# Edge counts of a graph layer in ten blocks of 125x125 a tile, three chunks a visit

## The reference

```
h = (x @ W.T).reshape(n, heads, out_ch)
e = leaky_relu(a_src[src] + a_dst[dst], 0.2)
m = segment_max(e, dst);  ex = exp(e - m[dst]);  denom = segment_sum(ex, dst)
out = segment_sum(ex / (denom[dst] + EPS) * h[src], dst)
x = x + gat2(relu(gat1(layernorm(x))));  x = x + ffn(layernorm(x))
```

## Time and profile before

| | us |
|---|---|
| median of 3 runs | 711.22 (710.97 to 712.07) |
| the profiled execution | 711.5 |
| its span | 709.7 |
| PE busy | 698.6 (98%) |
| DVE busy | 528.8 (75%) |
| ACT busy | 439.1 (62%) |
| POOL busy | 146.9 (21%) |

### The profile page before, as it was taken

The page is one execution under the profiler, slowest core; times in us unless marked ns, Lnnn a source line. Parts: engine busy times, 40 slices in busy tenths (PEclk is TensorE's granted clock), DMA queues, the critical chain, the costliest instruction groups (busy, mean ns, idle before and its releaser), DMA issues.

```text
span 709.7 us, 13757 instructions
## 1 busy us (share of the span) xinstructions
PE 698.6 (98%) x4705; PEld 655.6 (92%) x4705; DVE 528.8 (75%) x864; ACT 439.1 (62%) x898; POOL 146.9 (21%) x136
## 2 busy tenths in 40 slices
PE   8899999999999999999999999999999999999997
PEld 6699999888999999999999999999999899999997
DVE  5999888698999999999999664445568752737232
ACT  4665584387999999999999754553453333522202
POOL 2558121000112112121221000000223331323202
PEclk9999999999999999999999999999999999999999
DMA  8627887658633433443411431101882634315102
GB/s 285 215 69 199 255 249 218 183 148 247 199 71 76 94 69 84 81 99 59 92 21 21 123 116 59 59 0 37 253 276 64 207 92 189 102 57 178 44 23 66
DMA packets 48178, 88.35 MB, mean 124 GB/s; under 512 B 5263, under 2 KB 30831, under 8 KB 48128
## 3 DMA queue, kind: packets, MB, share of 16 engines
q1 hardware_dynamic: 37548, 65.69, 31.3%
q0 software_dynamic: 6080, 8.17, 7.4%
q10 hardware_dynamic: 4500, 13.82, 5.9%
HBM read 68.09 MB, written 15.33 MB: 118 GB/s over the span
## 4 chain that ended last, share of the span: by engine, by line
PE 90%; DVE 4%; DMA 4%; ACT 1%; issue 1%; POOL 0%; ACTq 0%; SPq 0%; DVEq 0%
PE bank L1479 19%; PE bank L1619 13%; PE bank L1440 12%; PE bank L1543 12%; PE bank L1336 11%; PE bank L1723 4%; DMA w1n_sb<-in_W 3%; PE bank L1695 3%; PE bank L1251 3%; PE bank L1597 2%; PE bank L1749 1%; DVE x2f L2359 1%; PE bank L1486 1%; PE bank L1485 1%; ACT w_hi L1035 1%; PE bank L1253 1%
## 5 line engine op out<-in xcount | busy, mean ns | idle before, releaser
L1479 PE MATMUL bank<-PT,h1s 125*128 125x250 f32 x660 | 147.5, 374 | 0.0
L1479 PEld LDWEIGHTS bank<-PT,h1s 125*128 125x128 f32 x660 | 121.2, 190 | 13.6
L2124 DVE SCALAR_TENSOR_TENSOR L<-asb,nad 125x1250 f32<-125x1250 f32 x80 | 121.3, 1551 | 2.5 <-DMA asb<-src_logit_rows 1.7
L2135 DVE CUSTOM_DVE_ANT_0 L<-L,LC 125x1250 f32<-125x1250 f32 x80 | 113.7, 1452 | 1.3
L950 ACT ACTIVATE L<-L,nm 125x1250 f32<-125x1250 f32 x80 | 109.7, 1373 | 7.1 <-DVE nm L2135 5.8
L1440 PE MATMUL bank<-ident,L 125*125 125x125 f32 x800 | 94.0, 273 | 0.0
L1440 PEld LDWEIGHTS bank<-ident,L 125*125 125x125 f32 x800 | 91.1, 189 | 0.8 <-issue 0.4
L971 ACT COPY PT<-bank 125x500 f32<-125x500 f32 x165 | 83.8, 616 | 1.9 <-PE bank L1440 1.9
L767 POOL DMA_DIRECT2D PT_diff<-PT x34 | 28.4, 836 | 157.9 <-ACT PT L971 157.9
L1932 DVE TENSOR_TENSOR hotr<-iota,r 125x1500 f16<-125x1500 f16 x50 | 46.6, 932 | 8.1 <-PE bank L1253 4.5
L1619 PE MATMUL bank<-h_hi,PT_hi 125*125 125x384 f32 x200 | 41.5, 350 | 0.0
(11 more groups left out here) (288 smaller groups left out, 1419.9 us busy)
## 6 DMA issues: line engine op xcount, KB each, us to landing
asb<-src_logit_rows SPq DMA_DIRECT2D x14, 416.5 KB, 3.5
atom_w<-in_atom_inT SPq DMA_DIRECT2D x5, 1152.0 KB, 12.6
atom_w<-in_atom_outT SPq DMA_DIRECT2D x5, 1152.0 KB, 9.7
log_count_scratch<-LCw SPq DMA_DIRECT2D x10, 546.9 KB
LC<-log_count_scratch SPq DMA_DIRECT2D x10, 546.9 KB
LCt<-log_count_scratch SPq DMA_DIRECT2D x10, 546.9 KB
h_scratch<-h1st ACTq DMA_DIRECT2D x10, 448.0 KB
PT_diff<-PT POOLq DMA_DIRECT2D x34, 122.1 KB, 3.0
```

The lines of the kernel that those rows point to most:

```text
L1479: mm = pe.matmul(sums, h1s[q][:, s, :], PT[p][:, s, :], start=(s == (0 if plain else PART + 2)), stop=(plain and s == NT - 1))
L2124: dve.scalar_tensor_tensor(L[s % RING][:, :], asb[q][0:NP, 1, :], nad1[:, ds(h, 1), t:t + 1].rearrange("p h t -> p (h t)"), asb[q][0:NP, 0 ...
L2135: dve.tensor_tensor_reduce(out=L[s % RING][:, :], in0=L[s % RING][:, :], in1=LC[:, t, :], scale=-1.0, scalar=-FLOOR, op0=ALU.add, op1=ALU.min,
```

## The change

A tile now has 10 blocks of 12 or 13 targets (`SUB` = 10; neighbours share the target at an odd edge), with row number target in block times 10 plus source divided by 125, and column number source modulo 125. Each block's counts are 125x125, a quarter of a bank. A visit makes two pairs of chunks and uses three of the four (`TRIP` = 2, `VISIT` = 3). The two tables become one, `edges`, one copy per tile parity, with four fp16 per chunk: row and column number, each of the chunk and of the chunk behind it. So a read may begin at any chunk, and the odd case on TensorE is gone. A block's first chunk is written as its place at even spread (`PLACE`) plus an offset of 0 to 3 chunks, two bits a block in the plan instead of four. The semaphores of the one-hots go by pairs of blocks (`HW` = 5). The count store writes 10 pieces of 125 numbers a partition. GpSimd fills both tables with -1 at the start; VectorE fills the row numbers twice per tile (`rows_of_edges`), and behind the one-hots of tile 0 also the column numbers of the second table.

```diff
-SUB = 5
+SUB = 10
+HW = SUB // 2
-WD = N // NW
-TRIP = 3
+WD = 13
+TRIP = 2
 VISIT = 2 * TRIP - 1
+PLACE = [w * NE // (CE * NW) for w in range(SUB)]
+LEAD = 16
-COLS = 2 * NCH + 4
+COLS = 2 * NCH + LEAD + 2
...
-        r16 = sb("r16", [CE, COLS], F16, p1)
-        g16 = [sb(f"g16_{p}", [CE, COLS], F16, p1) for p in range(2)]
-        hotk = [sb(f"hotk{w}", [CE, TRIP, NP, 2], F16, p1) for w in range(SUB)]
-        hotr = [sb(f"hotr{w}", [CE, TRIP, GW, 2], F16, p1) for w in range(SUB)]
+        edges = [None, sb("edges1", [CE, COLS, 2, 2], F16, p1)]
+        hot = [sb(f"hot{w}", [CE, 2, TRIP, NP, 2], F16, p1) for w in range(SUB)]
...
             for w in range(SUB):
-                pool.memset(sixteens[:, w:w + 1], float(16 ** w)).then_inc(consts_made, 1)
+                pool.memset(place[:, w:w + 1], float(PLACE[w])).then_inc(consts_made, 1)
+            for w in range(SUB):
+                pool.memset(fours[:, w:w + 1], float(4 ** w)).then_inc(consts_made, 1)
             for j in range(2):
                 pool.iota(iota2[:, :, j], pattern=[[1, SUB * NP]], ...)
...
+            for t in range(2):
+                pool.memset(edges[t][:, :, :, :], -1.0).then_inc(blank_set, 1)
...
                 with pe.Fori(0, count) as c:
-                    for w in range(SUB):
-                        out = bank[w // 2][0:NP, (w % 2) * GW:(w % 2 + 1) * GW]
-                        odd = ((start + (aways >> (4 * w)) + c) & 1).with_bounds(min_val=0, max_val=1)
-                        pe.wait_ge(hot_ready[w], before + c + 1)
-                        for q, j in ((0, 1), (1, 0), (1, 1), (2, 0)):
-                            pe.matmul(out, hotk[w][:, q, :, j], hotr[w][:, q, :, j], start=False, stop=True,
-                                      skip_group_check=True)
-                        mm = pe.matmul(out, end_of(hotk[w], odd), end_of(hotr[w], odd), start=False, stop=True,
-                                       skip_group_check=True)
-                        mm.then_inc(hot_used[w], 1)
+                    for v in range(HW):
+                        pe.wait_ge(hot_ready[v], before + c + 1)
+                        for w in (2 * v, 2 * v + 1):
+                            out = bank[w // 4][0:NP, (w % 4) * NP:(w % 4 + 1) * NP]
+                            for q, j in ((0, 0), (0, 1), (1, 0)):
+                                mm = pe.matmul(out, hot[w][:, 1, q, :, j], hot[w][:, 0, q, :, j], start=False, stop=True,
+                                               skip_group_check=True)
+                        mm.then_inc(hot_used[v], 1)
...
+            def place_of(t, kind, j):
+                return edges[t % 2][:, LEAD - j:LEAD - j + NCH, kind, j]
+
+            def rows_of_edges(t):
+                for j in range(2):
+                    s = dve.tensor_scalar(place_of(t, 1, j), gcol[:, :], -float(t * N), None, ALU.add)
+                s.then_inc(rows_set, 1)
...
                 with dve.Fori(0, count) as c:
-                    for w in range(SUB):
-                        away = ((aways >> (4 * w)) & 15).with_bounds(min_val=0, max_val=15)
-                        pair = ((start + away + VISIT * c) >> 1).with_bounds(min_val=0, max_val=COLS // 2 - TRIP)
-                        dve.wait_ge(hot_used[w], before + c + 1)
-                        dve.tensor_tensor(hotr[w][:, :, :, :],
-                                          iota2[:, 0:GW, :].unsqueeze(1).to_broadcast([CE, TRIP, GW, 2]),
-                                          r16[:, ds(2 * pair, 2 * TRIP)].rearrange("p (q j) -> p q j", j=2)
-                                          .unsqueeze(2).to_broadcast([CE, TRIP, GW, 2]), ALU.is_equal)
-                        dve.tensor_tensor(hotk[w][:, :, :, :],
-                                          iota2[:, w * NP:(w + 1) * NP, :].unsqueeze(1).to_broadcast([CE, TRIP, NP, 2]),
-                                          g16[t % 2][:, ds(2 * pair, 2 * TRIP)].rearrange("p (q j) -> p q j", j=2)
-                                          .unsqueeze(2).to_broadcast([CE, TRIP, NP, 2]), ALU.is_equal
-                                          ).then_inc(hot_ready[w], 1)
+                    for v in range(HW):
+                        dve.wait_ge(hot_used[v], before + c + 1)
+                        for w in (2 * v, 2 * v + 1):
+                            at = start + ((aways >> (2 * w)) & 3) + VISIT * c + PLACE[w]
+                            chunks = ds(at.with_bounds(min_val=0, max_val=COLS - 2 * TRIP), 2 * TRIP)
+                            for kind in range(2):
+                                made = dve.tensor_tensor(
+                                    hot[w][:, kind, :, :, :],
+                                    iota2[:, kind * w * NP:(kind * w + 1) * NP, :].unsqueeze(1).to_broadcast([CE, TRIP, NP, 2]),
+                                    edges[t % 2][:, chunks, kind, :].rearrange("p (q e) j -> p q e j", e=2)[:, :, 0, :]
+                                    .unsqueeze(2).to_broadcast([CE, TRIP, NP, 2]), ALU.is_equal)
+                        made.then_inc(hot_ready[v], 1)
+                if t == 0:
+                    dve.scalar_tensor_tensor(gcol[:, :], dstf[:, :], float(SUB), qc[:, :], ALU.mult, ALU.add
+                                             ).then_inc(edge_step, 1)
+                    for j in range(2):
+                        dve.scalar_tensor_tensor(place_of(1, 0, j), qc[:, :], -float(NP), srcf[:, :], ALU.mult, ALU.add)
+                    dve.wait_ge(edge_step, 5)
                 if t + 1 < NT:
-                    local_rows(t + 1)
+                    rows_of_edges(t + 1)
                     return plan_of(t + 1)
```

More of the change, by code:

```diff
@@ L252, in gnn_ffn_kernel @@
         vv = sb("vv", [NS, 2 * NW], F32, early)
-        vm = sb("vm", [2 * NW, 1], F32, early)
-        sixteens = sb("sixteens", [1, SUB], F32, early)
+        vm = sb("vm", [NW, 2], F32, early)
+        fours = sb("fours", [1, SUB], F32, early)
+        place = sb("place", [1, SUB], F32, early)
         nf = sb("nf", [1, NT, SUB], F32, early)
+        ends = sb("ends", [1, NT, SUB], F32, early)
         st = sb("st", [1, NT], F32, early)
@@ L297, in gnn_ffn_kernel @@
         xT_lo = [sb(f"xT_lo{p}", [128, KD, NP], F32R, p1) for p in range(2)]
-        xT_first = sb("xT_first", [128, KD, NP], F32, p1)
-        h1st = [sb(f"h1st{p}", [NP, HC], F32, p1) for p in range(2)]
+        edges[0] = sb("edges0", [CE, COLS, 2, 2], F16, p1)
+        pad_edges = sb("pad_edges", [CE, 32], F32, p1)
+        h1st = [sb("h1st0", [NP, HC], F32, p1)]
+        whole = ExitStack()
+        xT_first = sb("xT_first", [128, KD, NP], F32, whole)
+        whole.close()
+        h1st.append(sb("h1st1", [NP, HC], F32, p1))
         rows1 = sb("rows1", [H, 2, N], F32, p1)
@@ L411, in gnn_ffn_kernel @@
             sem(n) for n in ("span_step", "span_turned", "edge_step", "plan_ready"))
-        plan_step, g16_set = sem("plan_step"), sem("g16_set")
-        hot_ready = [sem(f"hot_ready{w}") for w in range(SUB)]
-        hot_used = [sem(f"hot_used{w}") for w in range(SUB)]
+        plan_step, rows_set, blank_set = sem("plan_step"), sem("rows_set"), sem("blank_set")
+        hot_ready = [sem(f"hot_ready{v}") for v in range(HW)]
+        hot_used = [sem(f"hot_used{v}") for v in range(HW)]
         cnt_full, ln_done, lc_done = (sem(n) for n in ("cnt_full", "ln_done", "lc_done"))
@@ L1902, in _ @@
             then(dve.scalar_tensor_tensor(trip[:, :], run[4][:, 8:18], 64.0, run[0][:, 9:19], ALU.mult, ALU.add))
[L1903 to L1904 removed]
+            then(dve.scalar_tensor_tensor(trip2[:, :], st[:, :], -2.0 ** 16, trip[:, :], ALU.mult, ALU.add))
             then(dve.tensor_tensor(offw[:, :, :], off[1][:, :, :],
[L1906 removed]
```

93 lines of the change are left out of this document (46 added, 47 removed).

## The result

The changed kernel takes 728.22 us (728.05 to 728.56, 4 runs) against 711.64 us (710.97 to 712.44, 4 runs): ratio 1.0233, 95% interval 1.0215 to 1.0251. It is slower by 16.6 us, where 8 us less had been forecast. The profiled execution has a span of 726.2 us.

A forecast was written before the change was run, and what follows sets the result against it. TensorE was taken to bound the kernel, VectorE close behind. 711.5 us less 9.6 for rounds and count 9, plus 1.5 for the later start, gave 703.4, or 703.1 against the median; range 699.8 to 710.3.

The forecast's parts named there:

- Counts: TensorE's count of a tile: 30 matmuls of 125 columns at 0.060 us, 2.0 us in all, 1.2 less than the mean.
- the rival with 0.081: TensorE's count matmuls run at the skill's distance of 0.081 us, rounds of 9.98, total 707.6 us; chance 0.12.
- One-hots: VectorE's one-hot loop: twenty instructions at 0.33 us, 6.55 a tile, nothing gained or lost; register work hides by 0.04 a block.
- Rounds: Eight rounds from count 1 to count 9: 9.40 us each instead of 10.56, a gain of 9.3 us.
- Start: VectorE's path to `wrow1` 2.6 us later, making TensorE's L1393 begin 1.5 later; bounds 0.5 and 3 us.
- GpSimd late with its two fills: At the start, doubled `iota2` and two memsets stand before `blank_set`, for which VectorE waits; a case for the 3 us bound.
- The upper bound of 3 us: Most that the later start was to cost TensorE, where 1.5 us was taken.
- GpSimd is starved: Rival: VectorE's gaps shrink, GpSimd's root for tile 8 holds up a turn once, up to 9 us; chance 0.06.
- the new row instructions may leave the access open: Reason against starved GpSimd: VectorE's new row-number instructions might let GpSimd into SBUF; no size given.
- Stores: Count stores in 1250 pieces of 500 bytes instead of 625 of 1000: DMA share 0.9 instead of 0.70, still hidden.
- the bound of 0.053: Count stores: a packet of 500 bytes was taken to last as long as one of 1000, 0.053 us.
- No second visit: One-hot blocks: each needs one visit as before; a second would cost its tile another 6.5 us of VectorE.

The follow-up runs named there:

- h_var: The changed kernel with each tile's variance and the scaled mean of tiles 8 and 9 computed by ScalarE instead of GpSimd: 713.48 us.
- o_added: `i_fast` with one tiny VectorE instruction, result unused, added behind `rows_of` of tiles 0 and 1: 704.84 us, ratio 0.9912.
- i_fast: `h_var` and `a_fill` together, with the second copy of `iota2` made by ScalarE and VectorE's work for tile 1 moved behind `watt1`: 715.74 us.
- a_fill: The changed kernel with GpSimd's two fills of the edge tables given to VectorE: 724.27 us.
- d_held_before: The kernel before, with four fills of 1250 numbers a partition added behind GpSimd's start-up work: 715.01 us, ratio 1.0039.
- n_gate_nmr: The changed kernel with eight VectorE waits for GpSimd's roots and one more for tile 8's scaled mean: 721.24 us.
- p_apart: `i_fast` with `rows_of` and `column_scaled` set apart on VectorE in the rounds of tiles 3 and 5 to 7: 720.45 us, ratio 1.0109.

## Why the prediction was wrong, point by point

- *Counts.* Forecast 0.060 us a pair and 2.0 a count. Measured 1.82 us for 30 pairs (53.10 to 54.92), 0.061, and 2.00 from 52.95 to 54.95. Right; the rival with 0.081 is out.
- *One-hots.* 0.33 apart and 6.55 a tile; measured 6.58 (54.77 to 61.35). No time to "issue" within the loop, so the register work hides. Right. (The elements per block fell to 1000 from 2250, four ninths and not the two fifths said under the change.)
- *Rounds.* 9.40, 75 to 76 us for eight. Measured 9.34 in the undisturbed ones, 75.8 in `h_var`, 75.94 in `o_added`. Right.
- *Start.* The path to `wrow1` was to be 2.6 later. It ends at 39.08 instead of 32.96, 6.1 later. The hold of L1857 is 3.5 of it (its successor begins at 8.80, in `i_fast` at 5.29), and 2.6 remain. That this equals the forecast is in part luck: VectorE begins L2059, the former L2038, 6.75 later, so the items took 3.2 (1.7 instead of 0.9 up to the one-hots of tile 0, 1.5 instead of 1.7 behind them), and 0.6 of it filled a wait that VectorE had for TensorE before L2042. The item that was missing is larger: "GpSimd late with its two fills" was thought of as VectorE waiting for `blank_set`, which was set in time. The fills did not have to be late to cost something: they kept GpSimd's queue unbroken while VectorE wanted in. That made 3.5 us on the path, and the lower clock behind TensorE's longer wait 4.5 more. Measured: 10.15 later at count 1, where 1.5 was taken. The upper bound of 3 us had no clock in it, though an idle TensorE was part of it.
- *GpSimd is starved.* This was the mechanism, and it had a chance of 0.06 and the price of one stall of 5 us. It was two stalls and 16.6 us. The step that failed is the reason against it, that "the same root under an idle moment took 0.55": the question was how many idle moments would be left. Before, VectorE waited for TensorE 0.76 to 1.77 us in each round from 75.73 on, and the one long root (44.37) falls into the stretch without such a wait. The forecast itself closed these waits, with both engines at 9.4, and still took the gain in full. The hope that "the new row instructions may leave the access open" was wrong as well: L720 waited from 52.27 past those at 61.35. The price counted one instruction late once; a tile needs two or three, and three in a row lost a round each (9.75, 9.44 and 9.77 us from 95.44 on).
- *Stores.* A store of 1237 packets took 49.9% of the 16 engines over 5 us (55 to 60), 0.032 us a packet of 500 bytes, less than the 0.053 of one of 1000, but a fifth more for the same bytes (66.5 us of engine time a MB instead of 55.6). The stage's DMA share is 0.80 and no engine waits for a store. Right that they hide; the bound of 0.053 was above the truth.
- *No second visit*: x30 in each of the counts. Right.

So 9.7 us of rounds were gained as forecast and 26.8 lost, 10.2 at the start and 16.6 in the rounds. The 16.6 are GpSimd's. Of the 10.2, 1.5 had been forecast from VectorE's own new work; 5.3 went in `a_fill` with 2.5 of the 3.5 us of hold. That VectorE and GpSimd shut each other out, and that this costs the time, is shown by `a_fill` and `d_held_before` for the start and by `h_var`, `n_gate_nmr`, `p_apart` and `o_added` for the rounds.

The Trainium skill (SBUF — State Buffer, Who interferes with whom) says that VectorE and GpSimd share a pair of ports, that an instruction of VectorE with two inputs from SBUF contends with a GpSimd instruction that reads there, and that the second to come is blocked until the first has finished. The trace agrees for the roots, which wait under one-hots with two inputs, that one is blocked, but not for how long: 19.25 and 39.6 us are dozens of VectorE's instructions of 0.4 us. These sentences do not cover the start: L1857 has one tensor as input and the fills have none, and yet it was held for 3.9 us, over five of GpSimd's instructions. So a queue without a break is often not entered between two of its instructions.

Often, not always. GpSimd in the kernel before, and VectorE beside it:

```profile
65.86 1.13 POOL L708 TENSOR_TENSOR rstd<-var,powers 125x1 f32<-125x1 f32 x1
66.96 0.97 POOL L706 TENSOR_SCALAR var<-mv 125x1 f32<-125x1 f32 x1
68.02 0.73 POOL L708 TENSOR_TENSOR rstd<-var,powers 125x1 f32<-125x1 f32 x1
```

```profile
66.50 0.54 DVE L1936 TENSOR_TENSOR hotk<-iota,g 125x750 f16<-125x750 f16 x1
66.96 0.93 DVE L1932 TENSOR_TENSOR hotr<-iota,r 125x1500 f16<-125x1500 f16 x1
```

Three instructions in a row got in within about a microsecond each, under one-hots without a gap, and three more from 98.23 to 100.88; the same loop had shut out the root of 44.37 for two tiles. So the idle moments that the change took away are not the whole account of why the kernel before was spared, and no run separates what the shape of the one-hots adds to it.

Open remains what makes such a place. All GpSimd instructions of over 5 us in the stage of the changed kernel and of `i_fast` ended at `rows_of` followed by `column_scaled`, or with VectorE idle. But one that came at 44.07 in `i_fast` ended at 45.67, at `rows_of` followed by `mend`, a sequence that did not let the next in at 55.2. And in `h_var` the root of 11.12 us ended at 81.41, between the first one-hots of tile 4, with neither of the two beside it. Whether PSUM as the source, the size of the next instruction or the state of VectorE's queue decides was not separated.

## What to carry to other kernels

Where two engines share an access, a busy share of 20% says nothing about the weaker one: count how many of its instructions a round needs, and how many openings the other engine leaves. A change that closes the last gaps of one engine has to be priced for all that lived in these gaps, however small. And a wait of TensorE costs more than its length where the clock falls behind it: 3.17 us of waiting were followed by work that took 4.5 us longer. It need not fall: in `o_added` TensorE waited 2.90 us for `w1n_sb`, the clock stayed at 1.00, and the next products ran 2.79 us.

## What was not expected of the hardware

- A waiting VectorE instruction is held through several back-to-back GpSimd instructions (3.9 us through five, 3.4 us through four fills put in for the purpose), not one.
- A GpSimd instruction on 125 numbers, tile 4's root, was held for 39.6 us in `p_apart`, and a useless VectorE instruction of 0.15 us at the right place released it ten us earlier than in `i_fast` (54.87, 64.80) and made the kernel 11 us faster in the median (715.74 to 704.84).
- Adding waits to the busiest helper engine made the kernel faster (`n_gate_nmr`, by 7 us).
- The granted clock was 0.50 from 39.14 to 48.00, while TensorE was without a gap, and 1.00 again later in the same unbroken stretch of work.
